# Graph network kernel: the place words of the bucket sums loaded one at a time instead of 28 at a time

## The reference, cut to what matters

```python
src = edge_index[0]
sums = jax.ops.segment_sum(edge_attr, src, num_segments=n)      # 100000 edges x 64 -> 6250 nodes x 64
counts = jax.ops.segment_sum(jnp.ones((edge_attr.shape[0],), edge_attr.dtype), src, num_segments=n)
edge_attr_agg = sums / jnp.maximum(counts, 1.0)[:, None]
combined = jnp.concatenate([x, edge_attr_agg, u_expanded], axis=1)
h = jax.nn.relu(combined @ W1 + b1)
return h @ W2 + b2
```

## Time and profile before

| | |
|---|---|
| median of 3 runs | 2984.27 us (2975.58 to 2985.07) |
| time of the profiled execution | 2979.5 us |
| its span, first to last instruction | 2977.7 us |
| mean granted TensorE clock | 0.848 of full speed |
| busy: PE, PEld | 2175.2 us (73%), 2005.6 us (67%) |
| busy: POOL, DVE, ACT | 2039.3 us (68%), 1892.7 us (64%), 970.0 us (33%) |
| products of the bucket sums (L2245) | 679.4 us to 1270.6 us |

### The profile page before, as it was taken

One profiled execution on the slowest core, in us unless ns is written; L12 is line 12 of the kernel. 1 busy time (PEld: TensorE's weight loads), 2 busy tenths in 40 slices (PEclk: granted clock), 3 DMA queues, 4 the chain that ended last, 5 costly groups with the idle time before them and its releaser, 6 DMA issues.

```text
span 2977.7 us, 48133 instructions
## 1 busy us (share of the span) xinstructions
PE 2175.2 (73%) x14401; PEld 2005.6 (67%) x14402; DVE 1892.7 (64%) x2801; ACT 970.0 (33%) x2710; POOL 2039.3 (68%) x1727
## 2 busy tenths in 40 slices
PE   0000037778888888799699995888988775699998
PEld 0000026657888888777599994777777664699998
DVE  8979987742323222356577676975555447698897
ACT  0000002220111111123366663555554441455553
POOL 5777777777777777401066663777777773678886
PEclk9999997885555555689899997999998888799999
DMA  6543345555444445312112223776777775423230
GB/s 211 151 122 90 97 109 152 150 150 130 115 119 116 110 115 132 95 60 74 54 32 57 57 59 100 192 195 190 189 193 194 190 194 156 112 67 91 64 98 32
DMA packets 332219, 358.48 MB, mean 120 GB/s; under 512 B 200434, under 2 KB 239216, under 8 KB 331828
## 3 DMA queue, kind: packets, MB, share of 16 engines
q1 hardware_dynamic: 210475, 196.63, 23.0%
q0 software_dynamic: 95744, 93.58, 13.7%
q10 hardware_dynamic: 25859, 66.47, 7.1%
HBM read 241.40 MB, written 122.94 MB: 122 GB/s over the span
## 4 chain that ended last, share of the span: by engine, by line
POOL 37%; PE 32%; issue 15%; DVE 12%; DMA 2%; ACT 1%; POOLq 0%; DVEq 0%; SPq 0%; ACTq 0%
POOL sorted L1155 30%; POOL mid L1231 6%; PE ps L2294 3%; PE ps L2394 3%; PE ps L2413 2%; PE ps L2272 2%; PE ps L2349 2%; PE ps L2351 2%; PE ps L2350 2%; PE ps L2371 2%; PE ps L2372 2%; PE ps L2370 2%; DVE yb L2125 1%; PE ps L2337 1%; PE ps L2540 1%
## 5 line engine op out<-in xcount | busy, mean ns | idle before, releaser
L1231 POOL DMA_INDIRECT mid<-h_rows,idx_a x400 | 486.0, 1215 | 131.0 <-issue 124.9
L2245 PE MATMUL ps<-big 128*128 128x65 f32 (+1 forms) x2380 | 493.1, 406 | 101.3 <-issue 82.2
L2245 PEld LDWEIGHTS ps<-big 128*128 128x128 f32 x2380 | 488.6, 320 | 107.2 <-issue 107.2
L1155 POOL DMA_INDIRECT sorted<-yb,idx_a x200 | 238.0, 1190 | 84.1 <-issue 60.7
L1583 DVE TENSOR_TENSOR big<-ps,big 128x1792 f32<-128x1792 f32 x85 | 171.6, 2020 | 176.4 <-PE ps L2245 163.9
L1164 POOL TENSOR_TENSOR rstd<-var,neg_half 125x2 f32<-125x2 f32 (+1 forms) x75 | 64.3, 858 | 316.0 <-DVE var L1638 315.8
L1155 POOL DMA_INDIRECT sorted<-wk,idx_a x200 | 238.3, 1191 | 61.0 <-issue 61.0
L1155 POOL DMA_INDIRECT sorted<-mid,idx_b x200 | 237.5, 1187 | 61.0 <-issue 60.6
L1155 POOL DMA_INDIRECT sorted<-xh,idx_b x200 | 237.4, 1187 | 61.0 <-issue 61.0
L1824 DVE TENSOR_TENSOR mid<-ps,xTg 128x256 bf16<-128x256 f32 (+1 forms) x245 | 122.3, 499 | 218.6 <-PE ps L2404 216.2
L1826 DVE TENSOR_TENSOR hT<-ps,mid 128x608 bf16<-128x608 f32 (+3 forms) x245 | 254.8, 1040 | 0.1
(11 more groups left out here) (381 smaller groups left out, 6312.0 us busy)
## 6 DMA issues: line engine op xcount, KB each, us to landing
h_in_r<-h_parts SPq DMA_DIRECT2D x245, 256.0 KB
big<-sorted ACTq DMA_DIRECT2D x85, 469.0 KB, 4.1
sorted<-hT SPq DMA_DIRECT2D x73, 469.0 KB, 7.4
mid<-in_L_ffn_w SPq DMA_DIRECT2D x16, 1024.0 KB
hid_x<-hT ACTq DMA_DIRECT2D x25, 500.0 KB
mid<-hid_x SPq DMA_DIRECT2D x25, 500.0 KB
h_parts<-h_part_r SPq DMA_DIRECT2D x24, 480.0 KB
mid<-h_rows,idx_a POOLq DMA_INDIRECT x400, 4.6
```

The lines of the kernel that those rows point to most:

```text
L1155: nc.gpsimd.indirect_dma_start(sorted_rows[c], bass.IndirectOffsetOnAxis(to_row[k][:, i:i + 1], 0), va[k][:, i, :], None).then_inc(s_put[k ...
L1231: nc.gpsimd.indirect_dma_start(mg4[:, s, i, :], None, h_rows, bass.IndirectOffsetOnAxis(idx4[:, s, i:i + 1], 0)).then_inc(s_gk[s], 16)
L2245: i_ = mm(banks[:, bass.ds(o_, w)], node_hot[:, s % 2, i, :], rows[:, i, 0:w], start=False, stop=True, skip_group_check=True)
```

## The change

The 28-word load at every fourth group goes. Instead, `places(j)` loads one word, with an instruction of its own. A group loads its word 0 before its waits; then, ahead of the two products of word j, it loads word j+1, until all 7 are loaded. So there are 85 x 7 = 595 loads of one word in place of 22 loads. The words, the shifts, the products and their order stay. Inside the loop each load's address depends on the turn, so a register holds it.

```diff
-LW = 4
...
-            held = []
-
             def bucket_sums(g, s=None):
                 s = g % NS if s is None else s
-                if s % LW == 0:
-                    n = min(LW, NGA - g) if isinstance(g, int) else LW
-                    _, held[:] = nc.values_load_multi_w_load_instructions(place_words[0:1, bass.ds(g * WP, n * WP)], engines=[pe.engine])
-                pairs = held[s % LW * WP:(s % LW + 1) * WP]
+                def places(j):
+                    return pe.value_load(place_words[0:1, bass.ds(g * WP + j, 1)])
+
+                pair = places(0)
                 wide = isinstance(g, int) and g >= WIDE_AT
...
                 for i in range(GA):
-                    o_ = pe.snap(pairs[i // 2] >> 12 if i % 2 else pairs[i // 2] & 4095)
+                    if i % 2 == 0:
+                        now, pair = pair, places(i // 2 + 1) if i < GA - 2 else None
+                    o_ = pe.snap(now >> 12 if i % 2 else now & 4095)
```

## The result

| | before | after |
|---|---|---|
| median | 2979.3 us (20 runs, 2975.58 to 2985.07) | 2986.4 us (20 runs, 2984.8 to 2989.34) |
| ratio | 1 | 1.0020 (95%: 1.0014 to 1.0027) |
| profiled execution, its span | 2979.5, 2977.7 us | 2986.3, 2984.5 us |
| wide groups, first product to end | 1230.4 to 1270.6: 40.2 us | 1232.5 to 1279.6: 47.1 us |
| from there to the end of the span | 1707.1 us | 1704.9 us |

The change costs 7.1 us. The predicted shift was 8.0; the predicted time, 2992.3, was 5.9 above the measured one, 5.0 of it because the median of three runs that it started from lies above the median of twenty.

The account below looks back on a forecast made before the run. GpSimd's scatters bound the bucket sums to 1221.4 us, then TensorE's nine wide groups. From 1230.1 us, 25.2 + 22.9 + 0.4 ends at 1278.6 instead of 1270.6: 2984.3 + 8.0 = 2992.3 us, range 2984 to 3004.

Parts of the forecast that it names:

- What bounds the stage: Bucket sums: GpSimd's scatters set the pace to 1221.4 us, covering the loop's 4.2 us holes; then TensorE's nine wide groups.
- The load holds its sequencer: TensorE's register loads: the sequencer does nothing else during a load, so loading one word ahead hides nothing.
- Rival E: Faster: the sequencer goes on during a load, the array sets the wide groups' pace, 31.3 us, -9 us; chance 0.08.
- Price of a load: One-word load on TensorE: 0.309 us plus a 0.06 us step, together 0.37; bounds 0.29 to 0.54.
- D: Rival of no change to speak of: at the bulk price of 0.29 us a load, +3 us; chance 0.13.
- Pace in the wide groups: Nine wide groups: the sequencer sets the pace, 2.8 + 7 x 0.37 = 5.4 us a group, above the warm array's 3.0.
- Rival B: The half clock stays on through the wide groups; the array takes 54.3 us there, +14 us; chance 0.12.
- Pace in the loop: Groups before the wide ones: sequencer 6.6 us a group, under the 7.25 at which TensorE would be late; worth 0.
- C: Rival: loop loads cost over 0.40 us, TensorE bounds the whole stage; +58 us at 0.484, +141 at 0.618; chance 0.08.
- A: The forecast case: wide groups bound by the sequencer, +4 to +12 us; chance 0.54.
- how much a measurement can tell: Whole kernel: resolution about 0.3%, 9 us; chances 0.44 slower, 0.49 within 0.3%, 0.07 faster.

Follow-up runs that it names:

- changed kernel's second trace: The changed kernel, unedited, run again on chip 2: median 3001.2 us against 2978.2 for the kernel before, ratio 1.0079; the traced execution took 3012.3 us.
- seven-word kernel: Against the changed kernel, one load of 7 words at the start of each group, everywhere; chip 2: median 2974.0 us, ratio 0.9990 to the kernel before.

## Why the prediction was right or wrong

**What bounds the stage: right.** The work before the last chunk is covered, the nine wide groups are on the path. Removing the 4.2 us holes bought nothing: TensorE waits 21.8 us for the last chunk instead.

**The load holds its sequencer: right.** Read from one load and one wait, confirmed by two words ahead (5.30 against 5.28 us a group) and by two words to a load (+15.2 us in the wide groups for 14.5 us of longer loads). Rival E falls.

**Price of a load: right, slightly high.** 0.309 assumed, 0.298 measured in the wide groups. The estimate of 0.299 from the line through 7 and 28 words was the better one, and D's bulk price, 0.234 without the fixed part, falls. The step after a load was read as below 0.14 us from two rounded times; they allow 0.19, and the trace has 0.064 there, so the 0.06 that was taken stands. The Trainium skill's floor of about 600 ns ("DMA: Bandwidth & Descriptors", section on latency and other measured facts) is not seen in any of these traces; its about 200 ns a register ("Runtime: NRT & Kernel Launch", section on instruction fetch mechanics) is nearer, with 234 measured, though that page speaks of registers loaded from HBM and these words lie in SBUF.

**Pace in the wide groups: right.** 2.8 + 7 x 0.37 = 5.4 us predicted, 5.3 measured; 8.0 us longer predicted, 6.9 measured. A load was 0.011 us cheaper than assumed, 62 x 0.011 = 0.7 us, most of the difference. The end came at 1279.6 for 1278.6, since the last chunk was complete 1.7 us later than before; the stages behind took 2.2 us less than before, and the whole is +6.8 us in the span.

**Rival B falls.** The clock stayed at 1.00 through products in fours with gaps of 0.2 us.

**Pace in the loop: right in this profile, with too little weight on what hangs on it.** Predicted 6.6 us a group, measured 6.4 back to back; the address instruction costs 46 ns and not 83. But the sum took the sequencer's and the array's pace and left out the ring from products over the count and the one-hot back to the products. Where counts came late, in the traces of chips 1 and 2, that ring set most of the 7.6 us a group, the cover was gone, and the same kernel lost 23 to 25 us instead of 7. Of that, C named the place (TensorE becomes late for the last chunk) but not the cause, for the loads cost no more there. So it is partly luck of the chip that the result lies inside A's +4 to +12 us: on two of the three chips timed afterwards it does not.

**The step that failed: how much a measurement can tell.** The text said that "a measurement tells this kernel from no change at about 0.3%, 9 us", put half the chance on "within 0.3%" and took what is left of A's +8 as hidden. Twenty runs of each kernel give 1.0014 to 1.0027, an uncertainty of 0.07% or 2 us, so +7 us is plainly slower. 9 us is about what lies between the lowest and the highest of the three runs shown (9.5); what two medians can tell is the uncertainty of their ratio, and that shrinks with the runs. With a resolution of 2 us, nearly all of A is slower, and so is D's +3; the likeliest outcome would have been "slower", from the same sum. The same three runs put the starting point 5.0 us too high.

**What stays open.** Why the counts come late on two of the chips and not in the result's run or on chip 3, and why more of them in kernels with many loads, was not settled. What ties them to GpSimd, and what speaks against GpSimd's transfers alone, stands below; neither shows a cause.

## What to carry to other kernels

A load into a register stopped TensorE's sequencer for its whole time (0.30 us for one word), so moving it "one ahead" hid nothing; put such loads where the engine waits for data anyway, and fetch many at once only if the pause falls there. Before crediting a removed hole, look at which stretch is on the chain: the larger hole here was covered, and the small price paid 62 times was not. Where an engine's slack is 10% of its pace, work out each ring of waits between engines as well as each engine's own sum, and time the kernel on more than one chip.

## What the runs showed of the hardware

**Register loads on TensorE.** From SBUF, 298 to 302 ns for one word, 532 for two, 1702 for seven and 6612 for 28: 234 ns a word and about 65 fixed. In the loop, beside the transfers, 28 words took 7281.

**The clock.** In the wide groups of the changed kernel it reads 0.50 from 1230 to 1236 us, 0.79 from 1236 to 1243 and 1.00 (2.4 GHz) from 1243 to 1277, with the array busy 6.19 of 7.00 us from 1250 to 1257.

**Late counts.** In the traces of chips 1 and 2 the count after a group reached its waiter up to 9.7 us after the start of the group's last product (up to 4.5 us with 28 words to a load); in the result's trace it took 0.43 us each time. The arrivals do not fall anywhere. GpSimd's transfers start every 1.49 us; in the changed kernel's second trace all 59 late counts that released VectorE, and in the seven-word kernel's all 54, came 0.42 to 0.62 or 1.18 to 1.37 us after such a start. In the result's trace the arrivals are spread evenly. That ties the delay to GpSimd's rhythm. But the transfers alone do not make a count late: in the changed kernel's second trace the counts up to 733 us came after 0.43 us, and in the seven-word kernel's those at 1197, 1203, 1209 and 1215 us too, while the transfers ran on to 1222 us at the same pace. The late ones lie between 740 and 1227 us in all these traces, close to the stretch in which ScalarE runs a loop of small copies with a register load each (L803, from 733 us; up to 1183 us in the seven-word kernel, whose last late count is at 1189, and up to 1217 in the changed kernel, whose last is at 1221). No run took the transfers or that loop away, so which of them it needs is open, and the difference between the chips has no explanation here. The medians of the kernel before are within 4 us on all three chips, for its ring has slack that the one-word loop used up.
